# Rows of units 2 to 4 by way of HBM and 32x32 transposes of VectorE, instead of transposes of TensorE

## The chip, the cores and the metric

The kernel runs on one core of one Trainium2 chip. The metric is the device time of one execution in microseconds (us), the median of the runs shown. PE is TensorE, ACT ScalarE, DVE VectorE, POOL GpSimd, SP SyncE.

## What is computed

Two attention layers, one behind the other, over two images of 32 x 32 = 1024 positions with 256 channels, in float32. Each layer is a group norm over 32 groups of 8 channels, a self-attention over the 1024 positions of an image, an output projection, and the sum with its input:

```python
def layer(x, gamma, beta, wq, bq, wk, bk, wv, bv, wp, bp):
    xn = group_norm(x, gamma, beta)
    q, k, v = conv1x1(xn, wq, bq), conv1x1(xn, wk, bk), conv1x1(xn, wv, bv)
    attn = softmax(einsum('bnc,bmc->bnm', q, k) / sqrt(C))
    out = einsum('bnm,bmc->bnc', attn, v)
    return conv1x1(out, wp, bp) + x
x = layer(x, ...layer 0, eps 1e-5); x = layer(x, ...layer 1, eps 1e-6)
```

## The kernel before

One pass of one layer over one image is a unit; there are four: unit 1 is image 0 in layer 0, unit 2 is image 1 in layer 0, unit 3 is image 0 in layer 1, unit 4 is image 1 in layer 1. In the code they are numbered u = 0 to 3, and `v` is the unit that is being prepared. The queries of a unit are two chunks of 512 columns; in the code chunk c belongs to unit c // 2, so a unit of the main loop has `before` = 2u - 1, `first` = 2u and `second` = 2u + 1.

Products that need float32 precision are sums of three products of split operands: a high part of type fp32r and the rest, a low part (`xn_hi`, `xn_lo`, `t_hi`, `t_lo`, `V`, `P_hi`, `P_lo`). For each unit PE makes, in this order: t = A xn (`t_product`, a half of the queries each, two of 6 matmuls), the values (`values`, 8 tiles of 6 matmuls), the scores of a chunk (`scores`, 8 tiles of 6 matmuls, 128 keys x 512 queries each), and the attention of a chunk (`attention`, 4 blocks of 128 queries, 8 x 3 matmuls each; these blocks are the j of `attend`). The loop is shifted: PE makes values(u), scores(first), blocks 0 and 1 of attention(before), the second half of t, blocks 2 and 3, scores(second), and then attention(first) with the first half of t of the next unit among its blocks.

The order on every engine is the order of the code; engines are held together by semaphores written out by hand. Each PE result goes to one of six banks in a fixed order (`ring_order`), and `wait_for_bank` lets PE reuse a bank when its reader of six places earlier is done. ACT copies each score tile to `S`; DVE keeps the maximum over key tiles in `R` (`running_max`), makes of it a shift for each query (`maxima_to_all`), adds it (`shifted`); ACT takes the exponentials twice (high part and full), POOL the low part (`p_low`). DVE's `output` scales a block of the attention and adds it to the residual rows in `xnat`.

What the next unit needs is prepared meanwhile. In `xnat` a row is a position; the products need channels on the partitions. So `next_rows` has PE transpose two row tiles (four 128x128 transposes, into the bank `Z`), ACT copies them to `xraw` (`raw_rows`), and DVE takes their statistics (`statistics_of`, `channel_statistics`). Two small matmuls average them over groups (`mean_of_groups`, `variance_of_groups`), with `group_deviation` and `variance` of DVE behind them; POOL takes the power -1/2 (`power`); DVE works out gain and shift (`affine_map`); `xraw` is scaled in four quarters (`normalise`), ACT rounds them (`xn_high`) and DVE or, from unit 3 on, POOL takes the rest (`xn_low`, `x_low`). The first half of t needs the low part of two quarters (`wait_for_x_low`).

Of the kernel before, what the change touches and what calls it, by code (L numbers as in the profile page):

```python
# [5 lines left out]
F32 = mybir.dt.float32  # L6
# [13 lines left out]
def two_attention_layers(nc, x, layers, vectors, out):  # L20
# [35 lines left out]
    TILES = 12  # L56
    P_TILES = 16
# [21 lines left out]
    for u in range(1, UNITS):  # L79
# [13 lines left out]
    ring_place = {tile: n for n, tile in enumerate(ring_order)}  # L93

    with ExitStack() as ctx:
# [21 lines left out]
        out_bias = sb("out_bias", [P, LAYERS, C])  # L117
        xraw = sb("xraw", [P, KC, N])
# [52 lines left out]
        ld_w = {(l, k): sem(f"ld_{k}{l}") for l in range(LAYERS) for k in ("wq", "wk", "wv", "wp")}  # L171
        ld_vec = sem("ld_vec")
# [43 lines left out]
        dv_att = sem("dv_att")  # L216
        dv_bn = sem("dv_bn")
# [33 lines left out]
        def _(sp):  # L251
# [21 lines left out]
            load_wide(1)  # L273
            load_image(1)

# [8 lines left out]
        def _(pool):  # L284
# [19 lines left out]
            def residual(u, i):  # L304

                pool.wait_ge(pe_xT, u * NR + i // 2 + 1)
                rows = xnat[:, u % IMAGES, i, :]
                nc.gpsimd.tensor_tensor(rows, rows, out_bias[:, u // IMAGES, :], ALU.add).then_inc(po_resid, 1)  # L308
# [55 lines left out]
        def _(act):  # L364
            act.dma_start(vec_rows[:], vectors).then_inc(ld_vec, 16)

            def raw_rows(v, r, bank):
                act.wait_ge(pe_xT, v * NR + r + 1)
                if v:
                    wait_for_x_low(act, v - 1, TQ)  # L370
# [28 lines left out]
            def xn_high(v, q):  # L399
# [3 lines left out]
                if v == 1:  # L403
                    act.wait_ge(ac_xn, q + 1)
                elif v and q >= KC:
                    act.wait_ge(ac_xn, TQ + (v - 2) * KC + q - KC + 1)
                else:
                    act.wait_ge(dv_xn, (TQ + (v - 2) * KC if v else 0) + q + 1)
# [5 lines left out]
            for r in range(NR):  # L414
                raw_rows(0, r, ring[2 + r % 2])
# [47 lines left out]
            for kb in range(NB):  # L463
                score_copy(0, kb)
                if kb < NR:
                    raw_rows(1, kb, Z)
# [20 lines left out]
            for u in range(1, UNITS):  # L487
# [8 lines left out]
                for kb in range(NB):  # L496
                    score_copy(first, kb)
                    if more and kb in (3, 6):
                        raw_rows(u + 1, kb // 3 - 1, Z)

                for kb in range(NB):
                    if kb in (3, 4):
                        t_high(u, 1, kb - 3)
                    if more and kb == 6:
                        raw_rows(u + 1, 2, Z)
                    exponentials(first, kb)

                for kb in range(NB):
                    score_copy(second, kb)
                    if kb == 0 and more:  # L510
                        raw_rows(u + 1, 3, Z)

                if more:
                    for q in range(KC):
                        xn_high(u + 1, q)
                    for q in range(KC, TQ):
                        normalise(u + 1, q)
                    for q in range(KC, TQ):
                        xn_high(u + 1, q)
                for kb in range(6):  # L520
                    if more and kb in (2, 3):
                        t_high(u + 1, 0, kb - 2)
# [6 lines left out]
        def _(dve):  # L529
# [11 lines left out]
            def statistics_of(v, r):  # L541
                dve.wait_ge(ac_xT, v * NR + r + 1)
# [145 lines left out]
            def maxima_to_all(c):  # L688
# [11 lines left out]
                dve.wait_ge(dv_fold, 7 * n + 2)  # L700

# [91 lines left out]
            for u in range(1, UNITS):  # L793
# [8 lines left out]
                for kb in range(1, NB):  # L802
                    running_max(first, kb)
                    if more and kb in (3, 6):
# [13 lines left out]
                output(before, 2)  # L818
                if more:
                    statistics_of(u + 1, 2)  # L820
                output(before, 3)

# [3 lines left out]
                running_max(second, 1)  # L826
                running_max(second, 2)
                if more:
                    group_deviation(u + 1)
                running_max(second, 3)  # L830
                if more:
                    variance(u + 1)
                running_max(second, 4)
                if more:
                    affine_map(u + 1)
                running_max(second, 5)
                if more:
                    normalise(u + 1, range(1))
                running_max(second, 6)
                if more:  # L840
                    normalise(u + 1, range(1, 2))
                running_max(second, 7)

                maxima_to_all(second)
# [7 lines left out]
                if more:  # L852
                    shifted(second, 2)
                    t_low(u + 1, 0, 0)
                    shifted(second, 3)
                    t_low(u + 1, 0, 1)
                    output(first, 2)
                    shifted(second, 4)
                    shifted(second, 5)
                    output(first, 3)  # L860
# [10 lines left out]
        def _(pe):  # L871
# [39 lines left out]
            def transpose_rows(bank, v, r):  # L911
                for k in range(KC):
                    for i in range(2):
                        last = nc.tensor.transpose(bank[:, (2 * k + i) * P:(2 * k + i + 1) * P],  # L914
                                                   xnat[:, v % IMAGES, 2 * r + i, k * P:(k + 1) * P], ident[:])
                last.then_inc(pe_xT, 1)

            def mean_of_groups(v):
                pe.wait_ge(ac_xT, v * NR + NR)
# [22 lines left out]
            for r in range(NR):  # L942
# [3 lines left out]
                transpose_rows(ring[2 + r % 2], 0, r)  # L946
# [86 lines left out]
            def next_rows(v, r):  # L1033

                if r == 0:
                    pe.wait_ge(dv_stat, (v - 1) * STAT + VARE)
                    pe.wait_ge(dv_ob, LAYERS)
                else:
                    pe.wait_ge(ac_xT, v * NR + r)
                if v < IMAGES:  # L1040
                    pe.wait_ge(ld_x[v][r], 16)
                else:
                    pe.wait_ge(dv_O, (v - IMAGES) * NB + 2 * r + 2)
# [149 lines left out]
```

## Time and profile before

| | |
|---|---|
| Median of 3 runs | 260.42 us (260.36 to 260.79) |
| Profiled execution | 260.44 us, of which the span of the trace is 258.4 us |
| PE busy | 252.5 us, 98% of the span |
| DVE, ACT, POOL busy | 183.7, 153.7, 125.9 us |
| Read from and written to HBM | 4.99 MB, 2.10 MB |

A time of the trace is counted from the start of the span. The profiled execution took 2.0 us more than its span, for what lies around it. Matmuls overlap in the trace, so what one costs is the distance of two starts, not its own length.

### The profile page before, as it was taken

To read this page: it belongs to the slowest core of one execution; us is meant where nothing else is said; L and a number is where in the kernel's file an instruction comes from. 1 tells how busy PE (TensorE), PEld (TensorE's weight loads), DVE (VectorE), ACT (ScalarE), POOL (GpSimd) and SP (SyncE) were. 2 spreads that over 40 slices of the span, in tenths; PEclk is the share of its full clock that TensorE was granted. 3 is DMA by queue.
4 is the path that set the end of the run, shared out by engine and by line. 5 is a ranking of instruction groups with operands and counts; after the bars stand their busy time and mean duration, and the time that the engine had idled before them with its cause. 6 is when DMAs were issued, how large, how long until landed. Compare 5 with 4: busy or idle time off the path is not lost.

```text
span 258.4 us, 4591 instructions
## 1 busy us (share of the span) xinstructions
PE 252.5 (98%) x1606; PEld 227.6 (88%) x1606; DVE 183.7 (71%) x481; ACT 153.7 (59%) x299; POOL 125.9 (49%) x151
## 2 busy tenths in 40 slices
PE   8999999999999999999999999999999999999995
PEld 7787789889988899889998899889998899889994
DVE  0588977788994598678766598778776488558804
ACT  3655644699984509746866418937667409840930
POOL 2010811386678407716756806815675906800870
PEclk9999999999999999999999999999999999999999
DMA  6960000000000000000000000000110001100112
GB/s 211 358 207 0 0 1 3 0 0 3 0 1 3 1 3 0 0 0 4 0 1 3 0 3 0 0 3 0 42 42 3 0 3 41 41 3 0 48 36 82
DMA packets 6990, 7.38 MB, mean 29 GB/s; under 512 B 556, under 2 KB 6712, under 8 KB 6968
## 3 DMA queue, kind: packets, MB, share of 16 engines
q1 hardware_dynamic: 6944, 7.08, 8.2%
q8 instruction: 13, 0.21, 0.3%
q14 instruction: 9, 0.07, 0.1%
q10 hardware_dynamic: 24, 0.01, 0.0%
HBM read 4.99 MB, written 2.10 MB: 27 GB/s over the span
## 4 chain that ended last, share of the span: by engine, by line
PE 69%; DVE 16%; ACT 7%; issue 5%; POOL 1%; DVEq 0%; ACTq 0%; POOLq 0%
PE ring L1027 10%; PE ring L1029 10%; PE ring L1028 10%; PE ring L1066 7%; PE ring L1068 7%; PE ring L1067 7%; DVE S L730 3%; PE ring L1013 3%; PE ring L1014 3%; PE ring L1015 3%; ACT S L456 2%; PE Z L914 2%; DVE xn_lo L626 2%; DVE xnat L740 2%; ACT P_hi L455 2%
## 5 line engine op out<-in xcount | busy, mean ns | idle before, releaser
L312 POOL TENSOR_TENSOR P_lo<-S,P_hi 128x512 fp32r<-128x512 f32 x64 | 82.1, 1306 | 66.1 <-ACT S L456 65.8
L1066 PE MATMUL ring<-V,P_hi 128*128 128x258 f32 x256 | 72.6, 283 | 0.0
L1068 PE MATMUL ring<-V,P_lo 128*128 128x258 f32 x256 | 72.4, 283 | 0.0
L1067 PE MATMUL ring<-V,P_hi 128*128 128x256 f32 x256 | 72.3, 282 | 0.0
L455 ACT ACTIVATE P_hi<-S 128x512 fp32r<-128x512 f32 x64 | 40.1, 627 | 36.2 <-DVE S L730 36.2
L448 ACT COPY S<-ring 128x512 f32<-128x512 f32 x64 | 37.5, 588 | 40.3 <-PE ring L1029 38.7
L1027 PE MATMUL ring<-t_hi,xn_lo 128*128 128x512 f32 x128 | 51.5, 402 | 0.0
L1029 PE MATMUL ring<-t_hi,xn_hi 128*128 128x512 f32 x128 | 50.0, 391 | 0.0
L1028 PE MATMUL ring<-t_lo,xn_hi 128*128 128x512 f32 x128 | 49.9, 390 | 0.0
L672 DVE TENSOR_TENSOR R<-ring,R 128x512 f32<-128x512 f32 x48 | 33.1, 690 | 22.7 <-ACT S L448 22.6
L1066 PEld LDWEIGHTS ring<-V,P_hi 128*128 128x128 f32 x256 | 48.5, 189 | 0.5
L1067 PEld LDWEIGHTS ring<-V,P_hi 128*128 128x128 f32 x256 | 48.4, 189 | 0.5
L1068 PEld LDWEIGHTS ring<-V,P_lo 128*128 128x128 f32 x256 | 48.5, 190 | 0.0
L730 DVE TENSOR_TENSOR S<-X,S 128x512 f32<-128x512 f32 x64 | 41.3, 681 | 0.0
L456 ACT ACTIVATE S<-S 128x512 f32<-128x512 f32 x64 | 39.7, 621 | 0.0
L308 POOL TENSOR_TENSOR xnat<-xnat,out_bias 128x256 f32<-128x256 f32 x32 | 23.0, 754 | 12.2 <-DVE out_bias L572 12.2
L1029 PEld LDWEIGHTS ring<-t_hi,xn_hi 128*128 128x128 f32 x128 | 24.0, 188 | 5.3
L1028 PEld LDWEIGHTS ring<-t_lo,xn_hi 128*128 128x128 f32 x128 | 24.1, 188 | 4.3
L1027 PEld LDWEIGHTS ring<-t_hi,xn_lo 128*128 128x128 f32 x128 | 24.1, 188 | 4.3
L661 DVE TENSOR_TENSOR V<-ring,V 128x256 fp32r<-128x256 f32 x32 | 13.4, 419 | 8.0 <-ACT V L441 7.9
L1013 PE MATMUL ring<-Wx_hi,xn_lo 128*128 128x258 f32 x64 | 18.6, 290 | 0.3 <-DVE xnat L740 0.3
L1014 PE MATMUL ring<-Wx_lo,xn_hi 128*128 128x258 f32 x64 | 18.1, 283 | 0.0
(116 smaller groups left out, 352.2 us busy)
## 6 DMA issues: line engine op xcount, KB each, us to landing
xnat<-in_x SPq DMA_DIRECT2D x8, 256.0 KB, 6.3
out<-xnat SPq DMA_DIRECT2D x16, 128.0 KB, 1.7
wide<-in_vectors SPq DMA_DIRECT2D x2, 384.0 KB, 6.9
w_wq<-in_L_conv_wq SPq DMA_DIRECT2D x2, 256.0 KB, 4.4
w_wk<-in_L_conv_wk SPq DMA_DIRECT2D x2, 256.0 KB, 4.6
w_wv<-in_L_conv_wv SPq DMA_DIRECT2D x2, 256.0 KB, 6.1
w_wp<-in_L_conv_wp SPq DMA_DIRECT2D x1, 256.0 KB, 5.6
w_wp<-in_L_conv_wo SPq DMA_DIRECT2D x1, 256.0 KB, 6.8
```

Of the source, the lines that this page charges most:

```text
L312: nc.gpsimd.tensor_tensor(P_lo[:, exp_of(c, kb), :], S[:, tile_of(c, kb), :], P_hi[:, exp_of(c, kb), :].bitcast(F32), ALU.subtract).then_i ...
L448: nc.scalar.copy(S[:, tile_of(c, kb), :], bank_of("S", c, kb)[:]).then_inc(ac_S, 1)
L455: nc.scalar.activation(P_hi[:, exp_of(c, kb), :], S[:, tile, :], ACT.Exp)
L456: nc.scalar.activation(S[:, tile, :], S[:, tile, :], ACT.Exp).then_inc(ac_P, 1)
L672: nc.vector.tensor_tensor(R[:], bank_of("S", c, kb)[:], earlier, ALU.max).then_inc(dv_R, 1)
L730: nc.vector.tensor_tensor(tile, X[:], tile, ALU.add).then_inc(dv_D, 1)
L1027: nc.tensor.matmul(bank[:], xn_lo[:, kc, keys], t_hi[:, kc, cols], start=(kc == 0), stop=False)
L1028: nc.tensor.matmul(bank[:], xn_hi[:, kc, keys], t_lo[:, kc, cols], start=False, stop=False)
L1029: last = nc.tensor.matmul(bank[:], xn_hi[:, kc, keys], t_hi[:, kc, cols], start=False, stop=(kc == KC - 1))
L1066: nc.tensor.matmul(bank[:, 0:C + 2], P_hi[:, tile, mine], v[:, kb, 0:C + 2], start=(kb == 0), stop=False)
L1067: nc.tensor.matmul(bank[:, 0:C], P_hi[:, tile, mine], v[:, kb, C + 2:VX], start=False, stop=False)
L1068: last = nc.tensor.matmul(bank[:, 0:C + 2], P_lo[:, tile, mine], v[:, kb, 0:C + 2], start=False, stop=(kb == NB - 1))
```

## The change

It replaces the PE transposes of units 2 to 4 (12 groups of four) and ACT's copies of them. The rows of image 1 are read from HBM a second time, those of layer 1 are stored by DMA to a tensor `between` in HBM as each output block is made, and both are read back into `moved` in pieces of 32 channels (128 bytes), so that each 32x32 block of `xraw` is the transpose of one block of `moved`. `nc.vector.transpose` does that for two row tiles at once (128 partitions x 512 elements) ahead of their statistics. The statistics, the group matmuls, the scaling and the first half of t of units 3 and 4 move to later places, and ACT does all four quarters of the scaling.

```diff
@@ ring order
-            ring_order += [("O", 2 * u, j) for j in range(2)]
+            ring_order += [("O", 2 * u, j) for j in range(3)]
             ring_order += [("t", u + 1, 0, k) for k in range(KC)]
-            ring_order += [("O", 2 * u, j) for j in range(2, QB)]
+            ring_order += [("O", 2 * u, 3)]
@@ SP
+            def load_moved(v, r, n=1):
+                source = x[v] if v < IMAGES else between[v - IMAGES]
+                pieces = source.rearrange("(t j) (k a c) -> k a j t c", j=SQ, k=KC, c=SQ)
+                place = moved[:, :, :, :, :].rearrange("p k i g c -> p k (i g) c")
+                tokens = slice(2 * QUARTERS * r, 2 * QUARTERS * (r + n))
+                for k in range(KC):
+                    for a in range(QUARTERS):
+                        sp.dma_start(place[a * SQ:(a + 1) * SQ, k, tokens, :], pieces[k, a, :, tokens, :]
+                                     ).then_inc(mv_x[v, r], 16)
+            load_moved(1, 0, NR)
             load_image(1)
+            for b in range(IMAGES):
+                for r, n in ((0, 2), (2, 1), (3, 1)):
+                    for i in range(2 * r, 2 * (r + n)):
+                        sp.wait_ge(dv_O, b * NB + i + 1)
+                        sp.dma_start(between[b, i * P:(i + 1) * P, :], xnat[:, b, i, :]).then_inc(st_x[b][i // 2], 16)
+                    sp.wait_ge(dv_turn, b * NR + r + n)
+                    for s in range(r, r + n):
+                        sp.wait_ge(st_x[b][s], 32)
+                    load_moved(IMAGES + b, r, n)
@@ ACT: raw_rows is gone for units 2 to 4
                 if more:
-                    for q in range(KC):
-                        xn_high(u + 1, q)
-                    for q in range(KC, TQ):
+                    for q in range(TQ):
                         normalise(u + 1, q)
-                    for q in range(KC, TQ):
-                        xn_high(u + 1, q)
+                        if q:
+                            xn_high(u + 1, q - 1)
+                    xn_high(u + 1, TQ - 1)
@@ DVE, statistics_of(v, r)
-                dve.wait_ge(ac_xT, v * NR + r + 1)
+                if v == 0:
+                    dve.wait_ge(ac_xT, r + 1)
+                else:
+                    if v > 1:
+                        wait_for_x_low(dve, v - 1, TQ)
+                    dve.wait_ge(mv_x[v, 0 if v == 1 or r == 1 else r], MOVED)
+                    nc.vector.transpose(xraw[:, :, 2 * r * P:2 * (r + 1) * P],
+                                        moved[:, :, 2 * r:2 * r + 2].rearrange("p k i g c -> p k (i g c)")
+                                        ).then_inc(dv_turn, 1)
+                    dve.wait_ge(dv_turn, (v - 1) * NR + r + 1)
@@ DVE, unit 1
-            for n in range(NATT):
-                attention_vector(1, n)
             for kb in range(1, NB):
                 running_max(0, kb)
+                if kb > NR:
+                    attention_vector(1, kb - NR - 1)
                 if kb <= NR:
                     statistics_of(1, kb - 1)
@@ DVE, main loop
-                    if more and kb in (3, 6):
+                    if more and kb in (4, 7):
                         statistics_of(u + 1, kb // 3 - 1)
...
+                for kb in range(1, 5):
+                    running_max(second, kb)
                 if more:
                     statistics_of(u + 1, 2)
+                running_max(second, 5)
+                running_max(second, 6)
                 if more:
                     statistics_of(u + 1, 3)
                     channel_statistics(u + 1)
+                running_max(second, 7)
                 if more:
                     group_deviation(u + 1)
+                maxima_to_all(second, statistics_again)
@@ PE, attention(c, ...)
                     for kb in range(NB):
                         attend(c, j, kb)
+                        if statistics and (j, kb) == (0, 6):
+                            mean_of_groups(c // 2 + 1)
+                        if statistics and (j, kb) == (1, 2):
+                            variance_of_groups(c // 2 + 1)
@@ PE
             for kb in range(NB):
                 scores(0, kb)
-                if kb < NR:
-                    next_rows(1, kb)
-                if kb == 6:
-                    mean_of_groups(1)
+            mean_of_groups(1)
...
-                attention(first, next_first_half, lambda: None)
+                attention(first, {2: next_first_half}, more)
```

`maxima_to_all` calls `statistics_again` (`variance` and `affine_map` of the next unit) behind its first reduction. POOL's `residual` waits for the store of its rows (`st_x`) instead of for PE's transposes.

Three places show how the order changes. The first is DVE in unit 1, from the second of the three `attention_vector` calls of layer 1 (`ISA products`, `ISA att`) to the first statistics behind the first running maximum (`R`). Before:

```order
L565 ISA products,att<-w_wk,wide 128x256
L565 ISA att 128x1
L565 ISA products,att<-wide 128x256
L565 ISA att 128x1
L672 TENSOR_TENSOR R<-ring,S 128x512
L544 BN_STATS bn<-xraw 128x6 x2
```

Now, from the call ahead of the first running maximum on:

```order
L592 TENSOR_TENSOR Wx_lo<-X,Wx_hi 128x256 x2
L705 TENSOR_TENSOR R<-ring,S 128x512
L572 STREAM_TRANSPOSE xraw<-moved 128x2x256
L577 BN_STATS bn<-xraw 128x6 x2
L705 TENSOR_TENSOR R<-ring,R 128x512
```

The products no longer stand ahead of the running maxima (they stand between the last three of them), and each pair of `BN_STATS` has a transpose ahead of it.

The second is DVE in unit 2, around the statistics of unit 3 that stand in its second chunk of queries (`R` is the running maximum of that chunk, the other names belong to unit 3). Before (the gain and the scaling of two quarters follow between the later maxima):

```order
L578 BN_AGGR mv<-bn 128x2 x2
L672 TENSOR_TENSOR R<-ring,S 128x512
L672 TENSOR_TENSOR R<-ring,R 128x512
L584 COPY gmean<-Z 128x2
L586 TENSOR_TENSOR dev<-mv,Z 128x2
L588 TENSOR_TENSOR dev<-dev 128x2
L590 TENSOR_TENSOR var_c<-dev,mv 128x2
L672 TENSOR_TENSOR R<-ring,R 128x512
L594 TENSOR_SCALAR var_e<-Z,eps 128x2
L672 TENSOR_TENSOR R<-ring,R 128x512
L601 TENSOR_TENSOR r0sq<-r 128x2
L603 SCALAR_TENSOR_TENSOR r_err<-r0sq,var_e 128x2
```

Now, from the fifth and sixth score tile's maxima on:

```order
L705 TENSOR_TENSOR R<-ring,R 128x512 x2
L572 STREAM_TRANSPOSE xraw<-moved 128x2x256
L577 BN_STATS bn<-xraw 128x6 x2
L611 BN_AGGR mv<-bn 128x2 x2
L705 TENSOR_TENSOR R<-ring,R 128x512
L617 COPY gmean<-Z 128x2
L619 TENSOR_TENSOR dev<-mv,Z 128x2
L621 TENSOR_TENSOR dev<-dev 128x2
L623 TENSOR_TENSOR var_c<-dev,mv 128x2
L729 STREAM_TRANSPOSE X<-R 128x512
L731 TENSOR_REDUCE folded<-X 128x16
L627 TENSOR_SCALAR var_e<-Z,eps 128x2
```

The last statistics stand behind the maximum of the seventh score tile instead of ahead of the first one, the group means behind the last maximum, and `var_e` and the gain behind the transpose and reduction of `R`.

The third is PE in attention(first) of unit 2: the small matmul of the group means, which stood among the scores of the second chunk, is now in block 0 of queries, behind its seventh key tile, where no other matmul stood.

```order
L1085 MATMUL ring<-V,P_hi 128x258
L1086 MATMUL ring<-V,P_hi 128x256
L1087 MATMUL ring<-V,P_lo 128x258
L953 MATMUL Z<-mv,group_mean 128x2
L1085 MATMUL ring<-V,P_hi 128x258
L1086 MATMUL ring<-V,P_hi 128x256
```

The matmul of the variances follows in block 1 behind its third key tile, and the 12 matmuls of the first half of t of unit 3, which stood behind block 1, stand behind block 2.

## Rows read from the trace of the kernel before

**Rows 1.** The page: busy time and share of an engine; granted clock in 40 slices.

```profile
PE 252.5 (98%) x1606; PEld 227.6 (88%) x1606; DVE 183.7 (71%) x481; ACT 153.7 (59%) x299; POOL 125.9 (49%) x151
...
PEclk9999999999999999999999999999999999999999
```

**Rows 2.** Timeline of PE, unit 1: start us, us, line, operation, idle before.

```profile
26.84 0.39 PE L1029 MATMUL ring<-t_hi,xn_hi 128*128 128x512 f32 x1
...
27.63 0.47 PE L1027 MATMUL ring<-t_hi,xn_lo 128*128 128x512 f32 x1
...
29.11 0.60 PE L914 MATMUL Z<-ident,xnat 128*128 128x128 f32 x4
29.46 0.48 PE L1027 MATMUL ring<-t_hi,xn_lo 128*128 128x512 f32 x1
...
46.17 0.39 PE L1027 MATMUL ring<-t_hi,xn_lo 128*128 128x512 f32 x1
```

**Rows 3.** Timeline of PE, first rows of five stages of unit 2.

```profile
89.90 0.28 PE L1066 MATMUL ring<-V,P_hi 128*128 128x258 f32 x1
...
104.68 0.40 PE L1027 MATMUL ring<-t_hi,xn_lo 128*128 128x512 f32 x1
...
116.95 0.28 PE L1066 MATMUL ring<-V,P_hi 128*128 128x258 f32 x1
...
122.71 0.39 PE L1000 MATMUL ring<-xn_hi,A_lo 128*128 128x512 f32 x1
...
131.23 0.28 PE L1013 MATMUL ring<-Wx_hi,xn_lo 128*128 128x258 f32 x1
```

**Rows 4.** Stage by stage: stretch, its length, granted clock, DMA share, GB/s.

```profile
16.00:17.00 1.00, 1.00 0.68 211
```

**Rows 5.** DMA queues, 3 to 4 us, then 10 to 11 us: packets, MB, share.

```profile
q1 hardware_dynamic: 321, 0.31, 90.6%
...
q1 hardware_dynamic: 182, 0.39, 108.5%
```

**Rows 6.** DMA issues: count, KB each, median us from issue to landing.

```profile
out<-xnat SPq DMA_DIRECT2D x16, 128.0 KB, 1.7
```

**Rows 7.** Timeline of ACT: copy of the second score tile of unit 1.

```profile
29.31 0.59 ACT L448 COPY S<-ring 128x512 f32<-128x512 f32 x1 [0.80 <-PE ring L1029]
```

**Rows 8.** Timeline of DVE, unit 1.

```profile
28.54 0.95 DVE L565 CUSTOM_DVE_ANT_0 products<-w_wk,wide 128x256 f32<-128x256 f32 x1
...
31.76 0.69 DVE L672 TENSOR_TENSOR R<-ring,R 128x512 f32<-128x512 f32 x1
32.37 0.74 DVE L544 BATCH_NORM_STATS2 bn<-xraw 128x6 f32<-128x256 f32 x2
...
40.97 0.42 DVE L661 TENSOR_TENSOR V<-ring,V 128x256 fp32r<-128x256 f32 x1
```

**Rows 9.** Timeline of DVE, unit 2.

```profile
102.32 0.75 DVE L654 SCALAR_TENSOR_TENSOR t_lo<-ring,att,t_hi 128x512 fp32r<-128x512 f32 x1 [0.27 <-ACT t_hi L434]
...
114.11 0.15 DVE L601 TENSOR_TENSOR r0sq<-r 128x2 f32<-128x2 f32 x1
...
115.16 0.69 DVE L672 TENSOR_TENSOR R<-ring,R 128x512 f32<-128x512 f32 x1
...
118.55 0.73 DVE L696 STREAM_TRANSPOSE X<-R 128x512 f32<-128x512 f32 x1
...
120.04 0.17 DVE L703 COPY X<-folded 64x16 f32<-64x16 f32 x1
```

**Rows 10.** Timeline of POOL, unit 2.

```profile
113.24 0.70 POOL L302 TENSOR_TENSOR r<-var_e,minus_half 128x2 f32<-128x2 f32 x1 [4.74 <-DVE var_e L594]
118.39 5.07 POOL L336 TENSOR_TENSOR xn_lo<-xraw,xn_hi 128x512 fp32r<-128x512 f32 x4 [4.45 <-ACT xn_hi L410]
```

**Rows 11.** Timeline of ACT, unit 2: quarters of the next unit.

```profile
118.73 1.52 ACT L396 ACTIVATE xraw<-xraw,shift,gain 128x512 f32<-128x512 f32 x2
120.16 1.12 ACT L410 CAST xn_hi<-xraw 128x512 fp32r<-128x512 f32 x2
```

More of the change, by code:

```diff
@@ L93, in two_attention_layers @@
     ring_place = {tile: n for n, tile in enumerate(ring_order)}
+    between = nc.dram_tensor("between", [IMAGES, N, C], F32, kind="Internal").ap()
     with ExitStack() as ctx:
@@ L117, in two_attention_layers @@
         out_bias = sb("out_bias", [P, LAYERS, C])
+        moved = sb("moved", [P, KC, NB, QUARTERS, SQ])
         xraw = sb("xraw", [P, KC, N])
@@ L171, in two_attention_layers @@
         ld_w = {(l, k): sem(f"ld_{k}{l}") for l in range(LAYERS) for k in ("wq", "wk", "wv", "wp")}
+        st_x = [[sem(f"st_x{b}_{r}") for r in range(NR)] for b in range(IMAGES)]
+        mv_x = {(v, r): sem(f"mv_x{v}_{r}") for v in range(1, UNITS) for r in range(NR)}
         ld_vec = sem("ld_vec")
@@ L818, in _, with statistics_again @@
                 output(before, 2)
+                output(before, 3)
+                def statistics_again():
+                    if more:
+                        variance(u + 1)
+                        affine_map(u + 1)
+                for kb in range(1, 5):
+                    running_max(second, kb)
                 if more:
                     statistics_of(u + 1, 2)
-                output(before, 3)
+                running_max(second, 5)
+                running_max(second, 6)
                 if more:
@@ L853, in _ @@
                     shifted(second, 2)
-                    t_low(u + 1, 0, 0)
                     shifted(second, 3)
-                    t_low(u + 1, 0, 1)
                     output(first, 2)
                     shifted(second, 4)
+                    output(first, 3)
+                    t_low(u + 1, 0, 0)
                     shifted(second, 5)
-                    output(first, 3)
+                    t_low(u + 1, 0, 1)
                 else:
@@ L1071, in attend, with attention @@
                     last.then_inc(pe_O, 1)
-            def attention(c, before_third, before_last):
+            def attention(c, behind, statistics=False):
                 pe.wait_ge(po_P, (c + 1) * NB)
@@ L1138, in _ @@
                     scores(first, kb)
-                    if more and kb in (2, 5):
-                        next_rows(u + 1, kb // 3)
-                attention(before, second_half, third_rows)
+                attention(before, {1: second_half})
                 for kb in range(NB):
                     scores(second, kb)
-                    if kb == 0 and more:
-                        next_rows(u + 1, 3)
-                    if more and kb == 2:
-                        mean_of_groups(u + 1)
-                    if more and kb == 4:
-                        variance_of_groups(u + 1)
-                attention(first, next_first_half, lambda: None)
+                attention(first, {2: next_first_half}, more)
             for kb in range(BY_KEYS):
```

87 lines of the change are left out of this document (27 added, 60 removed).

## The prediction

> **What bounds the kernel now.** First the page: PE is busy for 252.5 of 258.4 us, at a granted clock of full speed in every slice [rows 1]. So an edit gains only what it takes from PE's stream, and costs whatever it makes PE wait for. Then PE's timeline, stage by stage, for prices. In unit 1 the reader sees a score tile and a group of four transposes alternate: from 27.63 to 29.46 is one tile and one group, from 29.11 to 29.46 the group, and the matmul behind it is 0.08 longer than the usual 0.40 [rows 2]. So a group costs 0.44 and a tile 1.39. In unit 2, attention starts at 89.90, the scores of the second chunk at 104.68, the next attention at 116.95, its t at 122.71, the values at 131.23 [rows 3]. Two blocks of queries take 5.76, so one takes 2.88 and a key tile of it 0.36; 14.28 - 4 x 2.88 leaves 2.76 for half of t; a tile of values, 6 like matmuls, is 0.73.
>
> **What goes.** 12 groups x 0.44 = 5.3 us. Two places save more. In unit 1 the second tile starts at 27.63 and would start 0.23 behind 26.84, so 0.56 earlier [rows 2]. The scores from 104.68 to 116.95 take 12.27, and 8 x 1.39 is 11.1 [rows 3]: 1.2 for a group, what it waited, and two small matmuls that move into the attention. ACT's 12 copies were on no path of PE.
>
> **The loads.** Image 1 comes in 1024 x 8 = 8192 pieces of 128 bytes, 512 for each of 16 DMA engines. Its loads stand where those of image 1 stand now. The queue runs dry at about 16.7 [rows 4], and 1 MB at some 360 GB/s takes 2.9, so they start at about 13.8. No row shows such a piece. Between 3 and 4 us 321 packets of 1 KB took 90.6% of 16 us, 45 ns each; between 10 and 11 us 182 packets, many of 3 KB, took 95 ns at 2.1 KB each [rows 5]. A line through both gives 4 ns and 42 ns per KB, so 9 ns for a piece; from above, a piece costs no more than a whole packet, 45 ns. So the last lands between 19 and 38, with 1 us for the landing. DVE needs it at 29.9 (below), which is 29 ns a piece. I take 20 ns, 25 us, nearer to the line: it is hidden. For units 3 and 4 the first half (256 pieces an engine) starts a store's 1.7 us [rows 6] behind the last output of the chunk; at 20 ns it lands some 3 us before its transpose, and the last eighths, limited by eight issues, about 1 us before theirs.
>
> The Trainium skill ("DMA: Bandwidth & Descriptors", Specifications) says that a transfer below 512 bytes makes the DMA read, modify and write, and so speaks against these pieces. No run shown here has one of that size; by it a piece stands nearer to the upper bound, and the sum would be that of the first rival, up to 278.
>
> **Unit 1.** The copy of the second score tile ends at 29.90 [rows 7], now at 29.35. From there DVE is a chain. A running maximum is 0.61 (31.76 to 32.37), the statistics 0.75 [rows 8]; for the new transpose I take the one of the same 128x512 size, 0.73 and 0.03 to the next [rows 9] (from below it is 0.60, the distance of other passes of that size). Four times 2.12 is 37.8; the aggregation, two short instructions where six take 1.05 (114.11 to 115.16) [rows 9], ends at 38.15. Three maxima and three of the moved products of 0.88 [rows 8] follow: last maximum at 41.7, last product 42.55, `group_deviation` 43.1.
> PE ends its scores at 27.07 + 7 x 1.38 = 36.7 and now waits three times. `mean_of_groups(1)` waits for 38.15, 1.4 us. Three tiles of values end at 40.6, `maxima_by_query(0)` waits for 41.7, 1.1 us. Its transposes end at 42.15, `variance_of_groups(1)` waits for 43.1, 1.0 us. Behind it PE has five tiles of values and four transposes, 4.2 us, so its next scores start at 47.4 at least; before, DVE was this far at 40.97 [rows 8] and they started at 46.17 [rows 2], 5.2 later, so 48.3 at most. DVE's shift for the queries sets it; I take 47.8. **Term 1: +1.6 us** (+1.2 to +2.1), with the saving of four groups in it. What follows in unit 1 keeps its distances.
>
> **Units 2 and 3, each.** The groups among the first scores and blocks 2 and 3 give 3 x 0.44, the second scores 1.2: -2.5. DVE's last statistics of that first chunk, with a transpose, stand now behind its last maximum: 1.5 late. Everything to the second `t_lo` moves with it. That ended at 103.0 [rows 9] for scores at 104.68 (without a group 104.24): margin 1.3, so PE waits 0.2.
> Then the chain to the next t, counted from the start of attention(first), T. PE reaches the group means at 7 x 0.36 = T + 2.5; from a last matmul to its reader is 0.44 (28.87 to 29.31) [rows 2, 7]; four short DVE instructions end at T + 3.5. Transpose and reduction of `R` take 1.49 (118.55 to 120.04) [rows 9]: T + 5.0. `var_e`, 0.3, POOL's power 0.70 [rows 10]: T + 6.0. Six short ones: T + 7.1. ACT scales a quarter in 0.71 (118.73 to 120.16) and rounds one in 0.52 [rows 11], in the order scale, scale, round, scale, round: rounded quarters at T + 9.2 and 10.4. POOL takes 1.27 for each low part [rows 10]: T + 10.5 and T + 11.8. t waits for both. PE is there at 3 x 2.88 and two small matmuls, T + 8.9, and **stands for 2.9 us**. Values start at 11.85 + 2.76 + 2.88 = T + 17.5, where they started at T + 14.3: +3.2. The sum is -2.5 + 0.2 + 3.2 = +0.9 a unit, **term 2: +1.8 us**.
> Behind it ACT's exponentials are late by 5 us and its copies of the values with them. By my count the banks are freed 0 to 0.5 us before PE wants them, so small waits may come on top; I leave them at nothing. Unit 4 has no next unit.
>
> **Sum.** 260.44 (the profiled execution, 0.02 off the median) + 1.6 + 1.8 = **263.8 us**.
>
> **Rivals.**
> *Late loads.* If a piece costs a packet's 45 ns, image 1 lands at 38 instead of 29.9: PE is already waiting behind that chain, so all of 8 us counts. For units 3 and 4 the first half lands some 2.5 us late, and 2 x 3 us reach the scores through `t_lo`. Together 278. It decides from 29 ns a piece on, at 0.5 us per ns. Chance 0.17.
> *The clock falls.* PE idles for about 3 us at two places, and before for nothing like it; every slice shows the full clock, 2.4 GHz [rows 1]. If it fell to 1.2 behind each, every us of PE's work would cost one more; with 4 us of work behind each gap (my assumption) that is 2 x 4: 272. The Trainium skill ("TensorE: Matmul & The Clock Gate", Why this matters for your kernels) says that idle gaps between bursts of matmuls bring the clock down; the trace before has no such gap to try it on. Chance 0.08.
> *No wait at t.* The other side: the low parts are there when block 2 ends, since the group means or the two halves of the affine chain run earlier than I put them. Then 2 x 2.9 fall away: 258.0, faster. It decides where the chain from T to the second low part is shorter than 10.1 instead of 11.8 us. For it: half of t was put one block later, 2.88 us. Against it: every link has a row, and the means stand at a fixed place. Chance 0.09.
> *Small misses* in waits of 3.5 and 2 x 3.1 us could make it a tie, chance 0.06. My forecast, 262 to 266, has 0.60.
>
> **Numbers.** About 0.2% is what a measurement of this kernel can tell from no change (its runs spread by 0.16%). Slower by more: 0.60 + 0.17 + 0.08 = 0.85; within: 0.05; faster: 0.10. The range leaves out the far half of the late loads and most of the faster case: 260.8 to 270.
>
> **What would show it.** Right: 12 DVE transposes `xraw<-moved` near 0.75 us; PE waits of 1.4, 1.1 and 1.0 in unit 1; a wait near 3 us at the first matmul of t in units 2 and 3, released by POOL's `xn_lo`; `moved` landed before 29. Wrong: DVE waiting for DMA ahead of the transposes, PEclk below 9 behind a wait, or t without a wait. The most fragile part is the price of a piece, and after it the count of DVE's chain in unit 1.

## The result

The changed kernel takes 264.98 us, the median of 4 runs (263.86 to 265.76), against 260.39 (260.23 to 260.79) on the same chip: a ratio of 1.0169, 95% interval 1.0136 to 1.0202. It is 4.6 us slower, and the forecast was 263.8, slower by 3.4. The ratios here and below leave out two runs, of 354 and 407 us, whose mean granted clock was 0.66 and 0.56. The profiled execution took 265.76 us, its span 264.0, 5.6 more than before.

The page of the changed kernel, to compare with [rows 1]: PE's busy time and the granted clock.

```profile
PE 252.1 (95%) x1558; PEld 225.6 (85%) x1558; DVE 187.2 (71%) x489; ACT 150.4 (57%) x291; POOL 125.0 (47%) x151
...
PEclk9999999999999999999799999999889999999999
```

PE is busy as long as before, though 48 transposes are gone, and the clock has two dents. Both say the same: some of the busy time is matmuls at half speed. The waits of PE (engine, line, tile, what it waited for: us in all, times, longest):

```profile
PE ring L1032 <- POOL xn_lo L372: 5.0, 2, 2.5
PE Z L953 <- DVE mv L611: 1.2, 1, 1.2
```

5.0 us stand ahead of the first half of t of units 3 and 4 (`L1032`), where POOL's low parts of `xraw` are late, and 1.2 ahead of the group means of unit 2 (`L953`). The timeline of PE at the stages of [rows 2] and [rows 3] (start us, us, line, operation, idle before):

```profile
25.90 0.58 PE L1059 MATMUL ring<-t_hi,xn_lo 128*128 128x512 f32 x1
...
38.34 0.35 PE L953 MATMUL Z<-mv,group_mean 128*128 128x2 f32 x2 [1.16 <-DVE mv L611]
...
46.30 0.39 PE L1059 MATMUL ring<-t_hi,xn_lo 128*128 128x512 f32 x1
...
114.66 0.28 PE L1085 MATMUL ring<-V,P_hi 128*128 128x258 f32 x1
...
123.62 0.28 PE L1087 MATMUL ring<-V,P_lo 128*128 128x258 f32 x1
...
126.40 0.50 PE L1032 MATMUL ring<-xn_hi,A_lo 128*128 128x512 f32 x1 [2.50 <-POOL xn_lo L372]
...
130.42 0.42 PE L1085 MATMUL ring<-V,P_hi 128*128 128x258 f32 x1
...
133.71 0.28 PE L1045 MATMUL ring<-Wx_hi,xn_lo 128*128 128x258 f32 x1
```

And the first scores of unit 1 in the kernel before:

```profile
25.49 0.59 PE L1027 MATMUL ring<-t_hi,xn_lo 128*128 128x512 f32 x1
```

Stage by stage, as starts of PE's work in the two timelines. In unit 1 the scores start at 25.90, 0.4 later than before, and the next ones at 46.30 (46.17): the stage is 20.4 us, before it was 20.7. The 0.4 stand behind waits for the loads of image 0 and lie within the scatter: in the other traces of kernels with this start the first scores are between 25.2 and 26.8. Up to the start of attention(first) of unit 2, at 114.66 (116.95), the change gains another 2.4. Then comes what costs: from there to the values at 133.71 are 19.05 us, before 14.28 [rows 3], so 4.8 more, and unit 3 repeats it. The granted clock of that stretch (stretch, its length, PE busy and its matmuls, clock, DMA share, GB/s):

```profile
124.00:126.00 2.00, 0.00 (x0) 1.00 0.10 35
126.00:128.00 2.00, 1.60 (x7) 0.98 0.26 88
128.00:131.00 3.00, 3.00 (x10) 0.50 0.17 54
131.00:134.00 3.00, 3.00 (x26) 0.94 0.00 0
```

PE stands still, starts again at 126.40 at the full clock, 2.4 GHz, and 1.5 us later the clock goes to half, 1.2 GHz, for about 3 us. In the timeline above the 12 matmuls of t take 4.0 us to the start of the next block, not the usual 2.8. In unit 3 t starts at 188.19, and the clock falls about 1.2 us later.

### The profile page after: what moved, and what is told of

It is laid out like the page before. It is cut to its first block, busy times and chain, and to the rows that moved or that the text cites. A ratio compares the mean times of both kernels' runs of the same rounds, so it can differ in the third digit from the quotient of the medians.

```text
span 264.0 us, 4557 instructions
## 1 busy us (share of the span) xinstructions
PE 252.1 (95%) x1558; PEld 225.6 (85%) x1558; DVE 187.2 (71%) x489; ACT 150.4 (57%) x291; POOL 125.0 (47%) x151
## 4 chain that ended last, share of the span: by engine, by line
PE 65%; DVE 18%; issue 6%; ACT 6%; POOL 3%; DVEq 0%; ACTq 0%; POOLq 0%
PE ring L1059 9%; PE ring L1061 9%; PE ring L1060 9%; PE ring L1085 7%; PE ring L1087 7%; PE ring L1086 7%; PE ring L1045 2%; PE ring L1032 2%; PE ring L1046 2%; PE ring L1047 2%; PE ring L1034 2%; PE ring L1033 2%; DVE S L764 2%; POOL xn_lo L372 2%; DVE R L705 2%
## 5 line engine op out<-in xcount | busy, mean ns | idle before, releaser
L1059 PE MATMUL ring<-t_hi,xn_lo 128*128 128x512 f32 x128 | 50.6, 395 | 0.1
L333 POOL TENSOR_TENSOR r<-var_e,minus_half 128x2 f32<-128x2 f32 x4 | 2.8, 710 | 41.6 <-DVE var_e L627 41.6
```

The costliest lines, as they stand in the source:

```text
L1059: nc.tensor.matmul(bank[:], xn_lo[:, kc, keys], t_hi[:, kc, cols], start=(kc == 0), stop=False)
```

## Why PE waits at t

The chain to that t on three engines: DVE, then POOL, ACT and POOL again, in the order in which they hand over.

```profile
117.51 0.16 DVE L617 COPY gmean<-Z 128x2 f32<-128x2 f32 x1 [0.20 <-PE Z L953]
...
117.96 0.16 DVE L623 TENSOR_TENSOR var_c<-dev,mv 128x2 f32<-128x2 f32 x1
...
119.52 0.22 DVE L627 TENSOR_SCALAR var_e<-Z,eps 128x2 f32<-128x2 f32 x1
120.55 0.16 DVE L634 TENSOR_TENSOR r0sq<-r 128x2 f32<-128x2 f32 x1 [0.81 <-POOL r L333]
...
121.53 0.16 DVE L645 TENSOR_TENSOR shift<-vec_cols,gain_mean 128x2 f32<-128x2 f32 x1
...
133.91 0.17 DVE L770 RECIPROCAL row_inv<-ring 128x1 f32<-128x1 f32 x1 [4.68 <-PE ring L1087]
```

```profile
119.82 0.70 POOL L333 TENSOR_TENSOR r<-var_e,minus_half 128x2 f32<-128x2 f32 x1 [10.83 <-DVE var_e L627]
123.84 5.01 POOL L372 TENSOR_TENSOR xn_lo<-xraw,xn_hi 128x512 fp32r<-128x512 f32 x4 [3.32 <-ACT xn_hi L442]
```

```profile
123.16 0.60 ACT L442 CAST xn_hi<-xraw 128x512 fp32r<-128x512 f32 x1
...
124.38 0.60 ACT L442 CAST xn_hi<-xraw 128x512 fp32r<-128x512 f32 x1
```

With T = 114.66: the group means are read at T + 2.9, var_c is ready at T + 3.5, `var_e` stands behind transpose and reduction of `R` at T + 4.9, r0 is used at T + 5.9, the shift is made at T + 7.0, ACT has rounded the two quarters at T + 9.1 and 10.3, POOL has the second low part 2.5 us behind 123.84 (half of the 5.01 for four), at T + 11.7, and t starts at T + 11.74. PE had its last matmul of block 2 at 123.62. The last row of DVE shows the other end: it stands 4.7 us for block 3.

## Experiments

Each ran beside the kernel before; a ratio is to that. All but two are edits of the changed kernel; `unit2_only` and `before_products` are edits of the kernel before.

### unit2_only: the change for unit 2 alone

```diff
@@ kernel before, SP, ahead of load_image(1)
+            for k in range(KC):
+                for a in range(QUARTERS):
+                    pieces = x[1].rearrange("(t j) (k a c) -> k a j t c", j=SQ, k=KC, c=SQ)
+                    place = moved[:, :, :, :, :].rearrange("p k i g c -> p k (i g) c")
+                    sp.dma_start(place[a * SQ:(a + 1) * SQ, k, :, :], pieces[k, a, :, :, :]).then_inc(mv_x, 16)
@@ DVE, statistics_of(1, r): dve.wait_ge(mv_x, MOVED) and nc.vector.transpose(xraw rows, moved rows)
@@ ACT and PE, unit 1
-                    raw_rows(1, kb, Z)
-                    next_rows(1, kb)
@@ the products behind the last running maxima, mean_of_groups(1) behind the scores, as in the change
```

> The change for image 1 in layer 0 (unit 2) alone: its rows by the second read of x and DVE's transposes, products moved behind the last running maxima; units 3 and 4 keep PE's transposes and their order. Theory A (the loss is all in the prepared units 3 and 4, and unit 1's stage came out even because each moved product costs 0.34 us there and not 0.88): within 0.5 us of before, 260.2 to 260.9, with scores of the second chunk of unit 1 starting at about 46.3 and PE waiting once, 1.2 us, at the group means. Rival B (the term of my prediction: three waits in unit 1, net +1.6): 262.0.

259.98 us, median of 11 runs, against 260.59: ratio 0.9966 (0.9942 to 0.9990). PE's waits in it:

```profile
PE Z L942 <- DVE mv L596: 1.2, 1, 1.2
...
PE Z L932 <- DVE xnat L758: 0.5, 2, 0.3
```

The group means cost one wait of 1.2 us; the 0.5 are two waits ahead of transposes, which this kernel still has for units 3 and 4. Scores of the second chunk start at 45.76, 20.37 us behind the first ones. So this part of the change gains 0.3 us in its stage, and rival B, my term 1, falls. With this part the kernel is not slower than before, so the whole loss is in the preparation of units 3 and 4.

### before_products: only the three products moved

```diff
@@ kernel before, DVE, unit 1
-            for n in range(NATT):
-                attention_vector(1, n)
             for kb in range(1, NB):
                 running_max(0, kb)
+                if kb > NR:
+                    attention_vector(1, kb - NR - 1)
```

> The kernel before with the three products of layer 1 moved behind the last running maxima of unit 1, as the change has them. Theory A (they took 0.88 us each because POOL was adding the bias to the rows in the same stretch, from 26.9 to 33.0 us, and take 0.34 at their new place): 0.34 us each in the trace, POOL's eight additions 5.6 instead of 6.15 us, and no change of the time, since PE does not wait for them: 260.4. Rival B (their length has to do with the loads): 0.88 at the new place too.

260.67 against 260.59 (0.9985 to 1.0039): no change, as expected. All six products of the kernel (minimum, median and maximum ns, first and last start):

```profile
L565 DVE CUSTOM_DVE_ANT_0 products<-w_wk,wide x4: 412/418/421, 18.6 to 39.0; 128x256 f32<-128x256 f32 x4
L565 DVE CUSTOM_DVE_ANT_0 products<-wide x2: 415/415/415, 24.2 to 40.7; 128x256 f32<-128x256 f32 x2
```

In the kernel before, the three at 27.7 to 30.3 took 0.81 to 0.88 us each from start to start (one of them in [rows 8]), while POOL was adding the bias to the rows of unit 1:

```profile
26.90 6.15 POOL L308 TENSOR_TENSOR xnat<-xnat,out_bias 128x256 f32<-128x256 f32 x8 [12.23 <-DVE out_bias L572]
```

The same eight additions in before_products, with the products gone from beside them:

```profile
27.15 5.59 POOL L308 TENSOR_TENSOR xnat<-xnat,out_bias 128x256 f32<-128x256 f32 x8 [12.24 <-DVE out_bias L572]
```

At the new place POOL is idle; they are 0.42 us long and the next instruction starts 0.34 behind each. Their old length went with POOL's work beside them, and not with the instruction. Each slowed the other: POOL's additions are 0.56 us shorter without them. No load can be the neighbour, since the DMA share from 27 to 31 us of the kernel before is 0.00. Not every DVE instruction is slowed: the running maximum at 30.30, beside the same additions but with one input from a bank of PE, took its usual 0.68.

### warm and warm_11: matmuls that fill the wait

Matmuls on the identity, whose result nobody uses, stand behind block 2 and ahead of the first half of t of units 3 and 4; 20 of them, then 11.

```diff
                 def next_first_half():
                     if more:
+                        pe.wait_ge(dv_stat, (u + 1) * STAT + VARE)
+                        for _ in range(WARM):
+                            nc.tensor.matmul(Z[:, 0:P], ident[:], ident[:], start=True, stop=True)
```

> The changed kernel with 20 matmuls of 128 columns on the identity (their result is not used) put ahead of the first half of t of units 3 and 4, where PE waits 2.5 us; nothing else. Theory A (the wait itself lets the granted clock fall to 1.2 GHz, and that costs 1.8 us behind each of two waits): the wait shrinks to about 0.2 us, t starts at the same time as before, the granted clock stays at 1.00 and the kernel is 3 to 4 us faster than the changed one: 261.2, with less spread. Rival B (the low clock comes from something else, such as the kind of matmul, or costs nothing on the path): no change, 264.9. Rival C (the 20 matmuls are longer than the wait): t later by their excess, at most 0.5 us each.

265.91 against 260.59 (1.0156 to 1.0241), no faster than the changed kernel. Its timeline at that place:

```profile
123.09 4.63 PE L1148 MATMUL Z<-ident 128*128 128x128 f32 x40
127.47 0.48 PE L1033 MATMUL ring<-xn_hi,A_lo 128*128 128x512 f32 x1
```

20 matmuls stand in the trace as 40, 4.4 us in all: t starts at T + 13.5 instead of 11.7. The clock stayed at 1.00 in every run, and the kernel paid 1.7 us each for the surplus. That was rival C, larger than I had put it; hence the second size.

> As warm, with 11 matmuls instead of 20. In warm each took 0.22 us, so that 20 took 4.4 us against a wait of 2.5; 11 take 2.4. Theory A (the low clock behind the wait costs about 1.5 to 2 us at each of two places): t starts where it starts in the changed kernel, T + 11.8, the clock stays at 1.00, and the kernel takes 3 to 4 us less than the changed one, 261.3 with a narrow spread. Rival B (nothing is gained by the clock): 264.9.

262.34 against 260.43, ratio 1.0071 (1.0058 to 1.0083), the runs within 0.4 us, clock 1.00 in all. t and the values:

```profile
126.31 0.50 PE L1033 MATMUL ring<-xn_hi,A_lo 128*128 128x512 f32 x1
...
132.08 0.28 PE L1046 MATMUL ring<-Wx_hi,xn_lo 128*128 128x258 f32 x1
```

t starts at T + 11.75 (T = 114.56) as in the changed kernel; from t to the values is 5.77 us instead of 7.31. So with the same start of t the full clock is worth 1.5 us at each place, 3.1 by the rows and 2.6 by the medians of two kernels that were measured apart (264.98, 262.34). The clock falls because PE stands idle there, and that is a term of its own beside the wait.

### t_back: t where it stood before

```diff
-            ring_order += [("O", 2 * u, j) for j in range(3)]
+            ring_order += [("O", 2 * u, j) for j in range(2)]
@@ and its two fellows
-                attention(first, {2: next_first_half}, more)
+                attention(first, {1: next_first_half}, more)
```

> The changed kernel with the first half of t of units 3 and 4 back behind the second block of queries, where it stood before; all else as changed. Theory A (the chain of statistics sets when t can start, T + 11.8): the wait grows from 2.5 to 5.4 us, so 2 x 2.9 us more, and the clock stays low for about as long: 271. Rival B (the move of t is what delays things): faster than the changed kernel.

273.20 against 260.43, ratio 1.0487 (1.0470 to 1.0504). The wait at t, and the clock around it:

```profile
PE ring L1032 <- POOL xn_lo L372: 10.7, 2, 5.4
...
122.00:127.00 5.00, 0.00 (x0) 0.69 0.07 26
127.00:129.00 2.00, 1.82 (x4) 0.50 0.22 73
```

The waits are 5.4 each, as forecast: t starts when its chain is done, at T + 11.7 (127.18, T = 115.46), wherever it stands. The clock now falls inside the wait, at about 124, and stays down until about 130.7, twice as long as in the changed kernel. Half of that lies in the wait, where it costs nothing; the first 8 of the 12 matmuls of t run at half speed, and t takes 4.5 us (the next block starts at 131.67). From T to the values are 21.95 us in unit 2, 2.9 more than in the changed kernel, as forecast. The time is still 2.2 above the forecast of 271, and the traces place no part of that at t: the first scores start 0.9 later, within the scatter of the loads, and the values take 0.65 longer in each of units 3 and 4, about half of which the scores behind them give back. The rest may lie in the comparison of medians that were measured apart.

### act_order and chain: a shorter chain

First ACT's order alone, then three more links with it.

```diff
@@ act_order: ACT
                         normalise(u + 1, q)
-                        if q:
-                            xn_high(u + 1, q - 1)
-                    xn_high(u + 1, TQ - 1)
+                        xn_high(u + 1, q)
@@ chain: as act_order, and PE
-                        if statistics and (j, kb) == (0, 6):
+                        if statistics and (j, kb) == (0, 5):
-                        if statistics and (j, kb) == (1, 2):
+                        if statistics and (j, kb) == (1, 0):
@@ chain: DVE, maxima_to_all(c, meanwhile)
                 nc.vector.transpose(X[:], R[:]).then_inc(dv_fold, 1)
+                meanwhile[0]()          # variance(u + 1)
...
                 dve.wait_ge(dv_fold, 7 * n + 2)
-                meanwhile()             # variance and affine_map
+                meanwhile[1]()          # affine_map(u + 1)
```

> The changed kernel with ACT's order scale, round, scale, round for the four quarters instead of scale, scale, round, scale, round. Theory A (t waits for a chain DVE, ACT, POOL in which every link counts): the first rounded quarter comes 0.7 us earlier, POOL's second low part 0.7 to 0.8 us earlier, the wait at t falls from 2.5 to 1.7 us in both units, and the kernel is 1.5 us faster or more (263.4), more if the shorter wait also keeps the clock up (260 to 262). Rival B (t waits for something else, as its bank or the outputs): no change.

263.37 against 260.59, ratio 1.0121 (1.0078 to 1.0164). The wait is 2.17 us, not 1.7: a rounding that waits for the scaling right before it starts 0.9 us behind it, so a quarter takes 1.4 us, longer than POOL's 1.27 for a part, and POOL's second part waits for ACT. The profiled run shows both sides of the clock. Units 3 and 4, t and what follows it:

```profile
125.36 0.50 PE L1030 MATMUL ring<-xn_hi,A_lo 128*128 128x512 f32 x1 [2.17 <-POOL xn_lo L372]
...
128.24 0.28 PE L1083 MATMUL ring<-V,P_hi 128*128 128x258 f32 x1
...
185.31 0.51 PE L1030 MATMUL ring<-xn_hi,A_lo 128*128 128x512 f32 x1 [2.17 <-POOL xn_lo L372]
...
189.75 0.28 PE L1083 MATMUL ring<-V,P_hi 128*128 128x258 f32 x1
```

After the same wait the first t takes 2.9 us and the second 4.4; there the clock falls 0.4 us behind the start of t. Over its six runs the mean granted clock is 0.993 in four (262.9 to 263.5 us) and 0.987 in two (265.0 and 265.1): one fall, two falls. One more fall is 1.9 us. By the same count the changed kernel has two falls in its runs of 265.8 and 265.1 us (0.987 and 0.985) and one in those of 263.9 and 264.9 (0.993 and 0.992). So a wait of 2.5 us is not followed by a fall each time either, and the falls explain a part of that spread, not all of it.

> The changed kernel with a shorter chain to t: ACT scales and rounds in turn, the group means go behind the sixth key tile of block 0 and the variances behind the first key tile of block 1, and DVE adds eps between transpose and reduction of R, so that POOL's power runs beside the reduction. Theory A (every link counts): t starts at T + 10.5, the wait is 1.3 instead of 2.5 us, and if so short a wait leaves the clock alone, the kernel takes 2.4 + 3.5 us less than the changed one: 259.5, else 262.5. Rival B (it is the low parts of POOL alone that set it): no change from act_order, 263.4.

260.19 against 260.43, ratio 0.9987 (0.9977 to 0.9998). The wait in it:

```profile
PE ring L1034 <- POOL xn_lo L372: 2.4, 2, 1.2
```

1.2 us each, for a forecast of 1.3, and the clock is full in the nine runs that count. The time is 0.7 above the forecast of 259.5. From act_order to here the wait shrank by 2 x 1.0 and the time by 3.2; the rest is about the price of one fall of the clock, though the two ran on different chips.

### chain_low: a link given to another engine

```diff
@@ POOL
-                    for q in range(TQ):
+                    for q in (0, 2, 3):
                         x_low(u + 1, q)
@@ DVE
                 maxima_to_all(second, (variance_again, affine_again))
+                if more:
+                    xn_low(u + 1, 1)
```

> As chain, and DVE takes the low part of the second quarter (0.68 us, behind maxima_to_all) while POOL takes the first. Theory A: t starts at T + 9.7, the wait is 0.7 us, the clock stays at 1.00, and what the change saves on PE shows: 257.5 to 258.5, faster than before. Rival B (DVE reaches it late because its own chain is full, or the values wait later for banks): 259.5 or more.

259.29 against 260.43, ratio 0.9952 (0.9940 to 0.9965). DVE's low part and PE's t:

```profile
123.57 0.69 DVE L659 TENSOR_TENSOR xn_lo<-xraw,xn_hi 128x512 fp32r<-128x512 f32 x1 [0.60 <-ACT xn_hi L444]
...
124.36 0.47 PE L1038 MATMUL ring<-xn_hi,A_lo 128*128 128x512 f32 x1 [0.62 <-issue]
```

The wait is 0.6; the view names no releaser for it, but DVE's low part ends at 124.26. t starts at T + 9.93 (T = 114.43), 0.2 later than put. The kernel is now faster than before, by 1.1 us, but 0.8 short of the forecast.

### chain_banks, chain_mean, chain_values: the small waits

```diff
@@ chain_banks: DVE
+                    t_low(u + 1, 0, 0)
+                    shifted(second, 5)
+                    t_low(u + 1, 0, 1)
                     output(first, 3)
-                    t_low(u + 1, 0, 0)
-                    shifted(second, 5)
-                    t_low(u + 1, 0, 1)
@@ chain_mean: as chain_banks, and PE
                 scores(0, kb)
-            mean_of_groups(1)
             for m in range(NB):
                 values(0, m)
+                if m == 1:
+                    mean_of_groups(1)
@@ chain_values: as chain_mean, and ACT; kb in range(5) ahead of the values
-                    if m in (2, 5):
-                        exponentials(before, 6 + m // 3)
+                    if u == 1 and m in (2, 5):
+                        exponentials(before, 6 + m // 3)
+                    if u > 1 and m in (1, 3, 5):
+                        exponentials(before, 5 + m // 2)
```

> As chain_low, with DVE's two t_low of the next unit ahead of output(first, 3), for which DVE idled 1.0 us at 129.3, so that its shifted tile, ACT's exponential and the copies of the values behind it come earlier. Theory A (PE's small waits among the values and at the first two score tiles of units 3 and 4, together about 0.5 us a unit, are late banks, late because of that order): they go, 1.0 us in all, 258.3. Rival B (ACT's exponentials hold the copies up in any order): no change, 259.3.

259.54 against 260.57, ratio 0.9955 (0.9942 to 0.9968): nothing. Rival B was right, and I had read the idle DVE as the cause. Values to attention still take 17.5 us.

> As chain_banks, with the matmul of unit 2's group means behind the second tile of values of unit 1 instead of ahead of the first, where PE waits 1.2 us. Theory A (DVE's chain to the last running maximum sets the stage): the 1.2 us move to the next thing PE asks of DVE, the maxima behind the third tile of values, which wait for the last running maximum at 40.6 (in the changed kernel's time); 0.3 us are won at most, 258.0 to 258.3. Rival B (the wait was only one of order): 1.2 us less, 257.1.

259.02 against 260.57, ratio 0.9945 (0.9930 to 0.9959). The wait at the means became these two:

```profile
PE X L1078 <- DVE R L705: 1.1, 1, 1.1
...
PE Z L963 <- DVE var_c L623: 0.2, 1, 0.2
```

It moved to the running maximum (1.1 us) and the variances, as theory A has it. From the first scores to the next are 20.37 us (25.33 to 45.70), in chain_banks 20.40: nothing is won in this stage. The time is 0.7 above theory A's 258.3, and its interval overlaps that of chain_banks.

> As chain_mean, with ACT's exponential of the sixth score tile moved from ahead of the copies of the values of units 3 and 4 to behind the second of them (the seventh and eighth behind the fourth and sixth). Theory A (ACT is the one that frees PE's banks late: it works without a gap from 126 us to the first copy of the values): the first copy comes 1.0 us earlier and PE's small waits among values and first score tiles, about 0.5 us a unit, go: 258.0. Rival B (the later exponentials, which wait for DVE, then hold up the copies instead): no change, 259.0.

257.68 against 260.59, ratio 0.9891 (0.9873 to 0.9909). ACT's first copies of the values (`V`), in chain_mean and in this kernel:

```profile
133.29 0.90 ACT L475 CAST V<-ring 128x256 fp32r<-128x256 f32 x3
135.38 0.63 ACT L489 ACTIVATE P_hi<-S 128x512 fp32r<-128x512 f32 x1 [1.20 <-DVE S L765]
```

```profile
132.19 0.64 ACT L475 CAST V<-ring 128x256 fp32r<-128x256 f32 x2
132.70 0.65 ACT L489 ACTIVATE P_hi<-S 128x512 fp32r<-128x512 f32 x1
```

The first copy starts at 132.19 instead of 133.29, and DVE no longer keeps ACT waiting for 1.2 us at 135.38. Values and scores to attention take 16.7 us in unit 3 (129.62 to 146.31), against 17.4 in chain_mean (129.69 to 147.13): ACT's order freed the banks late. The gain, 1.3 us, is what theory A put at 1.0. The changed kernel itself takes 17.2 there (133.71 to 150.93). This is the fastest kernel of the study, 2.9 us under the kernel before.

## Why the prediction came out as it did

The forecast of 263.8 was right in sign, and 1.2 from the median, inside its range. That it is so near is luck: term 1 was 1.9 us too high and term 2 3.5 too low, and they hid each other. What was right as a mechanism is the wait at t, with its place, its length and its releaser.

**What goes.** Twelve groups and their waits, 2.5 us a unit in units 2 and 3. From 78.22 to 114.66 of the changed kernel are 36.4 us, before 38.9 (78.05 to 116.95): 2.5, and that includes the wait put at 0.2 at the second scores (103.63, 0.28 behind the matmul before it where 0.12 is usual).

**The loads** were hidden, as argued. DVE's first transpose follows its running maximum without a wait. The timeline of DVE in unit 1:

```profile
29.68 0.69 DVE L705 TENSOR_TENSOR R<-ring,S 128x512 f32<-128x512 f32 x1 [1.46 <-ACT S L480]
30.29 0.70 DVE L572 STREAM_TRANSPOSE xraw<-moved 128x512 f32<-128x512 f32 x1
31.02 0.75 DVE L577 BATCH_NORM_STATS2 bn<-xraw 128x6 f32<-128x256 f32 x2
...
40.53 0.42 DVE L598 CUSTOM_DVE_ANT_0 products<-wide 128x256 f32<-128x256 f32 x1
...
41.32 0.16 DVE L623 TENSOR_TENSOR var_c<-dev,mv 128x2 f32<-128x2 f32 x1
```

The new transpose is 0.70 long and 0.73 to the next instruction; I took 0.76. A piece shows here (queue 1 between 79 and 82 us, and the issues of unit 2 to landing):

```profile
q1 hardware_dynamic: 3022, 0.38, 79.4%
```

```profile
moved<-in_x SPq DMA_DIRECT2D x8, 128.0 KB, 4.0
```

3022 packets took 79.4% of 16 x 3 us, 12.6 ns each. My line through two sizes gave 9, the sum used 20, the packet's own bound was 45. The rival of late loads did not happen. The rule of the Trainium skill ("DMA: Bandwidth & Descriptors", Specifications), that transfers below 512 bytes are read, modified and written, does not show as a price near a whole packet's in this trace: the pieces are slow per byte and not per piece, 10 GB/s of an engine against 23 for the 1 KB packets of [rows 5].

**Term 1 (unit 1, +1.6)** was wrong; it measured -0.3. The step that failed is "three of the moved products of 0.88": 0.34 each at their new place. The last product ends at 40.9 and not 42.55, so of the three waits (1.4, 1.1, 1.0) only the first is there, 1.2 us, and DVE's four short instructions end at 41.5 instead of 43.1. The duration came from a row, but from a row with POOL at work beside it, and the instruction was moved away from that neighbour. before_products shows it.

**Term 2 (+0.9 a unit)** measured +2.5 in unit 2 (61.46 us from one unit's first scores to the next, before 58.94) and +2.8 in unit 3. The wait at t was named at its place, with its releaser, and at T + 11.85 for a measured T + 11.74; of 2.9 us the view shows 2.5. What was missing is mainly the clock, 1.5 us for each wait in the profiled run, and behind it the small waits named next. I had the clock as a rival of 0.08 with 4 us of slow matmuls each, since the trace before had no such gap. All four runs of the changed kernel have it at least once (clock 0.985 to 0.993), so the rival came true beside the forecast, at under half its price. The rule of the Trainium skill ("TensorE: Matmul & The Clock Gate", Why this matters for your kernels), that idle gaps bring the clock down, is borne out by the windows above and by warm_11, for waits of 2.5 us; behind the 1.2 us of chain the clock stayed up.

**Late banks.** "0 to 0.5 us" a unit, put at nothing; chain_values gained 1.3 us from chain_mean over two units, so they were real. In the changed kernel they are about 0.5 a unit, the upper end: 17.2 us from the values to the attention of unit 3, against 16.7.

**No wait at t**, the rival on the faster side, did not happen, but it named the place that decides. With the chain cut to 0.6 us of wait the change does win; only it was not the kernel that was made.

Left open: how much of the 2.6 us between the changed kernel and warm_11 belongs to their having been measured apart, and why the clock falls after one wait and not after another of the same length, in act_order at 2.17 us and, by its mean clocks, in the changed kernel at 2.5.

## What to carry to other kernels

Before a duration is moved with its instruction, look at what the other engines do in the stretch where it was measured, and in the stretch to which it goes. Work that is taken from the bounding engine is paid for by a chain on the others: write that chain as a list from its fixed start to its consumer, because wherever the consumer is put, it starts when the list ends. If the chain cannot be cut below the slack, price the wait together with the matmuls at half clock behind it, and try splitting the last link over two engines.

## What the runs showed of the hardware

- After waits of 2.5 and 2.17 us PE restarted at the full clock, 2.4 GHz, and in some cases, not in all, fell to 1.2 GHz 0.4 to 1.5 us later, for about 3 us. In a wait of 5.4 us (t_back) it fell inside the wait, for about 7. After 1.2 and 0.6 us (chain, chain_low) it did not fall, the one run of 407 us left aside. A fall cost 1.5 to 1.9 us.
- Twenty float32 matmuls of 128 columns stand in the trace as 40 and took 4.4 us, 0.22 each; four transposes of the same size stand as four and took 0.44, 0.11 each [rows 2].
- A 128-byte piece from HBM cost 12.6 ns of a DMA engine, a 1 KB packet 45 [rows 5].
- The same DVE product of 128x256 took 0.41 us with POOL idle and up to 0.95 with POOL's additions beside it, and POOL's eight additions took 6.15 us instead of 5.59.
